# A sparse attention kernel: the next group's lists made in mid-step, TensorE's chain work put ahead of its packing

## The chip, the cores and the metric

The program runs on one core of a Trainium2 chip. The metric is the device time of one execution in microseconds (us). The engines are named as in the profile: PE is TensorE (matmul), PEld its weight loads, DVE is VectorE, ACT ScalarE, POOL GpSimd and SP SyncE, which here only issues DMAs.

## The reference

One layer of graph attention over 8192 nodes with 256 features, 4 heads of 64, and a dense int32 adjacency matrix of 8192 x 8192 (256 MB) in which about 4 entries of a row are one:

```python
h = jnp.maximum(_layernorm(x), 0.0)
support = (h @ weight).reshape(-1, H, D).transpose(1, 0, 2)
f1 = jnp.einsum('hnd,hd->hn', support, weight_u[..., 0])[:, None, :]
f2 = jnp.einsum('hnd,hd->hn', support, weight_v[..., 0])[:, :, None]
masked = jax.nn.leaky_relu(f1 + f2, 0.2) * adj
mask = masked != 0
m = max over the masked entries of a row (0 if there are none)
e = jnp.where(mask, jnp.exp(masked - m), 0)
attn = e / e.sum(axis=2)            # 0 where the sum is 0
out = einsum('hnm,hmd->hnd', attn, support) + bias + h @ proj_w.T + proj_b
return x + out
```

## The kernel before

**The adjacency.** The rows are worked in 64 tiles of 128. SP loads a tile as four **units** of 1 MB (`load_adj`, L317) into a ring of six unit buffers (`HELD`); a new unit may be loaded when PE has used the one six before it (`s_adj_used`). Unit u of tile t is number 4t+u. PE packs each tile into 1024 words per row: two matmuls with a place code (`pack_places`, L392) and four for each unit (`pack_unit`, L400), into one of two PSUM tiles (`ps_words0`, `ps_two`). So a tile can be packed only when DVE has read the tile two before it out of the same PSUM tile. DVE's `pick_words` (L787 and on) takes the 16 largest words of each row; `split_words` (L799 to L813) turns them into neighbour numbers, 16 slots a row.

**First phase (to about 230 us).** For all 64 tiles of rows, layer norm and projections are computed, and the first 17 adjacency tiles (0 to 16) are packed and picked along the way.

**Second phase: steps.** The 64 row tiles are attended to in 32 groups of two. Step g (`for g in range(LATE)`, LATE = 30) has a part on each engine, in an order written out by hand. It works on three groups at once and picks the tiles `picks[g]`, in turn two (even g) and one (odd g) up to step 27, and two in each of steps 28, 29 and 30: step 26 picks 55 and 56, step 27 tile 57, step 28 tiles 58 and 59, step 29 tiles 60 and 61. The pieces, each named by its function:

- For group g+1: DVE `list_own` (L843 to L851; the first five neighbours of each row, and the count of the rest); PE `offsets` (L429, L430); ACT `distances` (L601 to L610).
- For group g: DVE `one_hot` (L859); PE `edge_records` (L438); ACT `record_edges` (L619); DVE `list_spill` (L867 to L877). The rows of a neighbour beyond five ("spill") are handed over by one-hot matmuls.
- For group g-1: DVE `scores` (L885 to L899) once its rows are gathered; PE `row_scores` (L445); DVE `row_maximum` (L908 to L914); PE `edge_refs` (L452); DVE `shift` (L922, L925); ACT `exponential` (L625); DVE `weigh` (L933).
- For group g-2: PE `aggregate` for each of its two tiles (L461, 12 matmuls each); DVE `output` (L939 to L943).

POOL gathers the neighbours' rows of 1040 bytes by indirect DMA (L717), 12 for each group: ten when `list_own` is there and ACT's `clear` (L592) has run, two after `list_spill`. The ring of gathered rows holds three groups.

**Order before the change.** PE in step g: `offsets(g)`; the first two units of the first new tile, which is one tile ahead of the pick; `aggregate(g-2, 0)`, `edge_records(g)`, `row_scores(g-1)`; the other two units; `edge_refs(g-1)`, `aggregate(g-2, 1)`; then the second new tile, if there is one. DVE in step g: pick of the first tile, `one_hot(g)`, `scores(g-1)`, `list_spill(g)`, `row_maximum(g-1)`, `output(g-2, 0)`, pick of the second tile, `shift(g-1)`, `split_words`, `list_own(g+1)`, `output(g-2, 1)`, `weigh(g-1)`.

**End.** The steps LATE and LATE+1 (30 and 31) are written out on their own: the last tile (63) is packed among the chain work of step 30, unit 1 before `aggregate(28, 0)`, unit 2 behind `aggregate(28, 1)`, and unit 3 behind `edge_refs(29)`. SP stores the output (L340) once the last adjacency load is issued.

Of the kernel before, what the change touches and what calls it, by code (L numbers as in the profile page):

```python
# [20 lines left out]
UNITS = 4  # L21
HELD = 6
GS = 2
RING = 3
FIRST = 16
# [18 lines left out]
def gat_kernel(nc, x, adj, weight, weight_u, weight_v, bias, proj_wT, proj_b, out):  # L44
# [4 lines left out]
    TILES = N // P  # L49
# [17 lines left out]
    picks = [list(range(FIRST + sum(counts[:g]), FIRST + sum(counts[:g + 1]))) for g in range(G + 2)]  # L67
    for g in range(1, G - 1):
        assert FIRST + sum(counts[:g]) >= groups[g][0] + groups[g][1]

    gathers = [sum(BLOCKS * groups[q][1] for q in range(g % RING, g + 1, RING)) for g in range(G)]

# [5 lines left out]
    with ExitStack() as ctx:  # L78
# [286 lines left out]
        def _(pe):  # L365
# [19 lines left out]
            def pack_places(t):  # L385

                if buffer_of(t) == 1 and t == FIRST + 1:
                    pe.wait_ge(s_staged, TILES)
                elif t > 0:
                    pe.wait_ge(s_words_seen, t if t <= FIRST else t - 1)  # L390
                for k in range(BANKS):
                    nc.tensor.matmul(ps_words[buffer_of(t)][:, k * 512:(k + 1) * 512], ones_row[:],  # L392
                                     place[:, k * 512:(k + 1) * 512], start=True, stop=False)

            def pack_unit(t, u):
                n = UNITS * t + u
                pe.wait_ge(s_adj_in[n % HELD], 16 * (n // HELD + 1))
                for s in range(UT):
                    for k in range(BANKS):
                        mm = nc.tensor.matmul(ps_words[buffer_of(t)][:, k * 512:(k + 1) * 512],  # L400
                                              pack_w[:, u * UT + s, :], adj_low[:, n % HELD, s, k * 512:(k + 1) * 512],
                                              start=False, stop=(u == UNITS - 1 and s == UT - 1))
                mm.then_inc(s_adj_used, 1)
# [20 lines left out]
            def offsets(g):  # L424
                first, size = groups[g]
                pe.wait_ge(s_spilled, g + 1)
                if g > 0:
                    pe.wait_ge(s_rec_sb, g)
                nc.tensor.matmul(ps_list[:, 0:size], before[:], spilled[:, first:first + size], start=True, stop=True)  # L429
                nc.tensor.matmul(ps_list[:, GS:GS + size], minus_mid[:], spilled[:, first:first + size],  # L430
                                 start=True, stop=True).then_inc(s_offset, 1)

            def edge_records(g):
                first, size = groups[g]
                pe.wait_ge(s_onehot, g + 1)
                pe.wait_ge(s_filed, g + 1)
                for b in range(size):
                    mm = nc.tensor.matmul(ps_rec[:, b], onehot[:, g % 2, b], record[:, first + b, OWN:R_F1],  # L438
                                          start=True, stop=True)
                mm.then_inc(s_rec, 1)  # L440
# [14 lines left out]
            def aggregate(g, b):  # L455
                if g > 0:
                    last, n = groups[g - 1]
                    pe.wait_ge(s_out, last + min(b, n - 1) + 1)
                pe.wait_ge(s_weighted, groups[g][0] + b + 1)
                for k in range(BLOCKS):  # L460
                    mm = nc.tensor.matmul(ps_agg[:, b, 0:ROW], ident[:] if k < OWN else onehotT[:, g % RING, b],  # L461
                                          gathered[:, g % RING, b, k], start=(k == 0), stop=(k == BLOCKS - 1))
                mm.then_inc(s_agg, 1)

            pe.wait_ge(s_staged, TILES)
            for g in range(LATE):
                new = [t + 1 for t in picks[g]]
                offsets(g)
                pack_places(new[0])
                for u in range(UNITS // 2):  # L470
                    pack_unit(new[0], u)
                if g >= 2:
                    aggregate(g - 2, 0)
                edge_records(g)
                if g > 0:
                    row_scores(g - 1)
                for u in range(UNITS // 2, UNITS):
                    pack_unit(new[0], u)
                if g > 0:
                    edge_refs(g - 1)  # L480
                if g >= 2:
                    aggregate(g - 2, 1)
                for t in new[1:]:
                    pack_places(t)
                    for u in range(UNITS):
                        pack_unit(t, u)

            offsets(LATE)
            pack_places(TILES - 1)
# [64 lines left out]
        def _(act):  # L554
# [41 lines left out]
            def distances(g):  # L596
                first, size = groups[g]
                act.wait_ge(s_spilled, g + 1)
                if g > 0:
                    act.wait_ge(s_onehot, g)  # L600
                nc.scalar.activation(reach[:, 0:size], spilled[:, first:first + size], ACT.Square, scale=0.5)  # L601
                nc.scalar.activation(slot_pen[:, g % RING, 0:size], held[:, 0:size], ACT.Copy, scale=-NEG,
                                     bias=NEG).then_inc(s_slot_pen, 1)
                act.wait_ge(s_offset, g + 1)
                n = step(nc.scalar.activation(mid[:, 0:size], ps_list[:, GS:GS + size], ACT.Copy))
                nc.scalar.activation(record[:, first:first + size, R_OFF], ps_list[:, 0:size],
                                     ACT.Copy).then_inc(s_filed, 1)
                act.wait_ge(s_act, n)
                for b in range(size):
                    last = nc.scalar.activation(distance[:, b], edge_odd[:], ACT.Square, scale=0.5,  # L610
                                                bias=mid[:, b:b + 1])
                last.then_inc(s_distance, 1)
# [16 lines left out]
            for g in range(LATE):  # L629
                record_edges(g)  # L630
                if g == 0:

                    for b in range(2):
                        act.wait_ge(s_rows_out[b], 16 * (LOADS // 2))
                    act.wait_ge(s_xhat, TILES)
                    act.wait_ge(s_xT, TILES)
                    act.wait_ge(s_based, TILES)
                    for q in range(RING):
                        clear(q)
                if g > 0:  # L640
                    exponential(g - 1)
                if g + 1 >= RING:
                    clear(g + 1)
                distances(g + 1)

            clear(LATE + 1, 0, 1)
            record_edges(LATE)
# [97 lines left out]
        def _(dve):  # L745
# [36 lines left out]
            def pick_words(t, at):  # L782

                ps = ps_words[buffer_of(t)]
                dve.wait_ge(s_adj_used, UNITS * (t + 1))
                for s in range(CANDS // 8):
                    last = v.max(cand[:, s * 8:(s + 1) * 8], ps[:, s * SEG:(s + 1) * SEG])  # L787
                last.then_inc(s_words_seen, 1)
                dve.wait_ge(s_words_seen, t + 1)
                v.tensor_tensor(seg_top[:], seg_top[:], cand[:, 7::8], ALU.max)  # L790
                after(step(v.max(words[:, at, 0:8], cand[:])))
                after(step(v.match_replace(cand_rest[:], words[:, at, 0:8], cand[:], 0.0)))
                return step(v.max(words[:, at, 8:16], cand_rest[:]))
# [61 lines left out]
            def one_hot(g):  # L855
                size = groups[g][1]
                dve.wait_ge(s_distance, g + 1)
                for b in range(size):
                    last = v.tensor_scalar(onehot[:, g % 2, b], distance[:, b], reach[:, b:b + 1], None, ALU.is_lt)  # L859
                last.then_inc(s_onehot, 1)  # L860
# [85 lines left out]

            list_own(0)
            for g in range(LATE):
                n = pick_words(picks[g][0], 0)
                if g == 0:  # L950

                    dve.wait_ge(s_based, TILES)
                one_hot(g)
                if g > 0:
                    scores(g - 1)
                list_spill(g)
                if g > 0:
                    row_maximum(g - 1)
                if g >= 2:
                    output(g - 2, 0)  # L960
                for t in picks[g][1:]:
                    n = pick_words(t, 1)
                if g > 0:
                    shift(g - 1)
                picked = split_words(picks[g][0], len(picks[g]), n)
                list_own(g + 1)
                if g >= 2:
                    output(g - 2, 1)
                if g > 0:
                    weigh(g - 1)  # L970
# [152 lines left out]
```

## Time and profile before

| | us |
|---|---|
| median of 3 runs | 863.06 |
| lowest, highest | 859.76, 864.25 |
| the profiled execution | 860.12 |
| its span, first to last instruction | 858.4 |

The busy time of each engine over the span: PE 710.9 us (83%), DVE 643.1 (75%), POOL 529.0 (62%), ACT 129.3 (15%). The DMA engines moved 329.82 MB, 384 GB/s in the mean. In a row of the timeline the two numbers ahead are start and duration in us; the bracket is the time for which the engine sat idle before, and what ended it.

### The profile page before, as it was taken

The numbers are of one execution on the slowest core, as the hardware profiler recorded it, in microseconds if no ns is written. First come the engines' busy times: TensorE is split into PE (matmuls) and PEld (weight loads), VectorE is DVE, ScalarE is ACT, GpSimd is POOL, SyncE is SP. The second block draws the span as 40 slices with busy tenths as digits, with TensorE's granted clock in tenths as the row PEclk, the third lists the DMA queues.
The fourth block names the chain that finished last, engine by engine and source line by source line (L and its number), as shares of the span: only waits on it lengthen the run. The fifth ranks groups of instructions, "written<-read, shape, count | busy, mean of one in ns | idle before, by whom it ended". The sixth has DMA issues, their size and how long they took to land.

```text
span 858.4 us, 11157 instructions
## 1 busy us (share of the span) xinstructions
PE 710.9 (83%) x3011; PEld 434.2 (51%) x3011; DVE 643.1 (75%) x2740; ACT 129.3 (15%) x467; POOL 529.0 (62%) x598
## 2 busy tenths in 40 slices
PE   2989999999956878887888888788888878888865
PEld 0656666666513545454555445354544445454454
DVE  4556666657446988879869798977979787886887
ACT  0223333333210111000001011000011100000010
POOL 4344455454467776667766667676766766676570
PEclk9999999999966989888879898887989888988789
DMA  9999999999999999999999999999999999999971
GB/s 307 422 407 393 416 422 416 407 423 413 419 410 384 385 401 402 388 405 384 402 393 374 399 374 405 383 404 384 390 396 375 406 366 400 359 403 401 397 302 53
DMA packets 63855, 329.82 MB, mean 384 GB/s; under 512 B 12795, under 2 KB 15560, under 8 KB 31024
## 3 DMA queue, kind: packets, MB, share of 16 engines
q1 hardware_dynamic: 43056, 286.28, 83.8%
q0 software_dynamic: 18432, 34.30, 11.1%
q10 hardware_dynamic: 2304, 8.52, 2.4%
q8 instruction: 25, 0.41, 0.2%
q14 instruction: 38, 0.31, 0.1%
HBM read 328.99 MB, written 16.91 MB: 403 GB/s over the span
## 4 chain that ended last, share of the span: by engine, by line
PE 42%; DMA 25%; DVE 24%; issue 4%; POOL 3%; ACT 1%; POOLq 0%; ACTq 0%; SPq 0%
DMA adj_raw<-in_adj 21%; PE ps_words L400 11%; PE ps_agg L461 9%; PE ps_agg L381 7%; PE ps_two L381 6%; DVE att L933 5%; PE ps_two L400 5%; DVE cand L787 3%; DVE base L943 3%; POOL att L717 2%; DMA att<-support_table,idx 2%; PE ps_score L445 2%; DMA att<-in_x 1%; PE ps_words L392 1%; DMA support_table<-att 1%
## 5 line engine op out<-in xcount | busy, mean ns | idle before, releaser
L717 POOL DMA_INDIRECT att<-support_table,idx x384 | 417.4, 1087 | 188.7 <-issue 105.8
L400 PE MATMUL ps_words<-adj_raw,pack_w 128*128 128x512 fp8e4 x640 | 186.7, 428 | 25.4 <-DMA adj_raw<-in_adj 25.3
L461 PE MATMUL ps_agg<-att,ident 128*128 128x260 f32 x640 | 176.3, 428 | 8.5 <-DVE att L933 8.5
L461 PEld LDWEIGHTS ps_agg<-att,ident 128*128 128x128 f32 x640 | 135.1, 218 | 41.6 <-issue 18.6
L400 PE MATMUL ps_two<-adj_raw,pack_w 128*128 128x512 fp8e4 x384 | 118.9, 457 | 24.6 <-DMA adj_raw<-in_adj 24.5
L400 PEld LDWEIGHTS ps_words<-adj_raw,pack_w 128*128 128x128 bf16 x640 | 62.1, 106 | 125.3 <-DMA adj_raw<-in_adj 39.8
L787 DVE MAX8 cand<-ps_words 128x8 f32<-128x128 f32 x320 | 67.1, 281 | 66.3 <-PE ps_words L400 66.3
L933 DVE TENSOR_TENSOR att<-att 128x1536 f32<-128x1536 f32 x64 | 109.4, 1750 | 0.4 <-ACT att L625 0.4
L708 POOL COPY record<-att 128x8 f32<-128x8 f32 x64 | 13.4, 209 | 117.4 <-ACT att L569 117.4
L400 PEld LDWEIGHTS ps_two<-adj_raw,pack_w 128*128 128x128 bf16 x384 | 38.7, 113 | 91.5 <-DMA adj_raw<-in_adj 40.0
L381 PE MATMUL ps_agg<-w_all,hT 128*128 128x260 f32 x256 | 63.0, 389 | 4.1 <-ACT hT L565 4.1
L381 PE MATMUL ps_two<-w_all,hT 128*128 128x260 f32 x256 | 62.6, 388 | 3.0 <-ACT hT L565 3.0
L943 DVE SCALAR_TENSOR_TENSOR base<-ps_agg,rdenom,base 128x64 f32<-128x64 f32 x256 | 55.0, 277 | 2.3
L381 PEld LDWEIGHTS ps_two<-w_all,hT 128*128 128x128 f32 x256 | 47.8, 192 | 11.9 <-ACT hT L565 3.5
L381 PEld LDWEIGHTS ps_agg<-w_all,hT 128*128 128x128 f32 x256 | 46.0, 190 | 13.5 <-ACT hT L565 7.9
L706 POOL TENSOR_TENSOR base<-att,bias_row 128x256 f32<-128x256 f32 x64 | 46.8, 732 | 0.1
L710 POOL TENSOR_TENSOR base<-base,att 128x256 f32<-128x256 f32 x64 | 46.6, 729 | 0.0
L867 DVE TENSOR_SCALAR edge_slot<-edge_rec,edge_at 128x2 f32<-128x2 f32 x32 | 7.8, 245 | 51.2 <-ACT edge_rec L619 51.2
L787 DVE MAX8 cand<-ps_two 128x8 f32<-128x128 f32 x192 | 40.2, 280 | 6.6 <-PE ps_two L400 6.5
L619 ACT ACTIVATE edge_rec<-ps_list 128x34 f32<-128x34 f32 x32 | 6.4, 199 | 243.3 <-PE ps_list L438 243.2
L445 PE MATMUL ps_score<-score_slot,onehotT 128*128 128x44 f32 x128 | 24.6, 331 | 19.7 <-DVE score_slot L899 19.6
L625 ACT ACTIVATE att<-shifted 128x24 f32<-128x24 f32 x64 | 10.7, 215 | 189.9 <-DVE shifted L925 189.9
(118 smaller groups left out, 821.2 us busy)
## 6 DMA issues: line engine op xcount, KB each, us to landing
adj_raw<-in_adj SPq DMA_DIRECT2D x256, 1024.0 KB, 13.3
support_table<-att ACTq DMA_DIRECT2D x16, 520.0 KB, 8.8
att<-in_x SPq DMA_DIRECT2D x16, 512.0 KB, 6.7
out<-base SPq DMA_DIRECT2D x15, 512.0 KB, 14.1
att<-support_table,idx POOLq DMA_INDIRECT x384, 6.2
out<-base SPq DMA_DIRECT2D x4, 128.0 KB, 1.9
w_all<-in_proj_wT SPq DMA_DIRECT2D x2, 128.0 KB, 6.0
w_all<-in_weight SPq DMA_DIRECT2D x2, 128.0 KB, 6.3
```

The lines of the kernel that those rows point to most:

```text
L381: mm = nc.tensor.matmul(ps_proj[t % 2][:, half, 0:ROW], hT[:, t % 2, c * P:(c + 1) * P], w_all[:, c, half, :], start=(c == 0), stop=(c == ...
L400: mm = nc.tensor.matmul(ps_words[buffer_of(t)][:, k * 512:(k + 1) * 512], pack_w[:, u * UT + s, :], adj_low[:, n % HELD, s, k * 512:(k + 1 ...
L445: mm = nc.tensor.matmul(ps_row[:, b].rearrange("p k h -> p (k h)"), onehotT[:, g % RING, b], score_slot[:, b].rearrange("p k h -> p (k h)" ...
L461: mm = nc.tensor.matmul(ps_agg[:, b, 0:ROW], ident[:] if k < OWN else onehotT[:, g % RING, b], gathered[:, g % RING, b, k], start=(k == 0) ...
L625: last = nc.scalar.activation(gathered[:, g % RING, b, :, HF:], shifted[:, b], ACT.Exp)
L706: pool.tensor_tensor(base[:, t], x_in[:, g % 2, q, :], bias_row[:], ALU.add).then_inc(s_basev, 1)
L708: pool.tensor_copy(record[:, t, R_F2:].rearrange("p (a h) -> p a h", a=2), stage[:, g % 2, :, q, HF:])
L710: pool.tensor_tensor(base[:, t], base[:, t], stage[:, g % 2, 0, q, 0:HF], ALU.add).then_inc(s_based, 1)
L717: pool.indirect_dma_start(gathered[:, g % RING, b, k, :], None, table, bass.IndirectOffsetOnAxis(idx[:, g % RING, b, k:k + 1], 0), bounds_ ...
L787: last = v.max(cand[:, s * 8:(s + 1) * 8], ps[:, s * SEG:(s + 1) * SEG])
L933: v.tensor_tensor(r, r, rows[:, :, HF:].unsqueeze(3).to_broadcast([P, BLOCKS, H, HD]), ALU.mult).then_inc(s_weighted, 1)
L943: last = v.scalar_tensor_tensor(base[:, t, cols], ps_agg[:, b, cols], rdenom[:, b, h:h + 1], base[:, t, cols], ALU.mult, ALU.add)
```

## The change

DVE makes the list of the next group (`list_own(g+1)`) in the middle of a step instead of near its end, and `one_hot(g)` is the first thing in a step; PE makes `offsets(g+1)` in step g, and ACT the distances ahead of the exponential. This holds for the groups in `AHEAD`, which the formula makes groups 1 to 26; groups 0 and 27 to 29 keep the old place, and steps 30 and 31 are as before. PE packs tile 17 before the first step, and in every step does all the chain work first and then packs the tiles two ahead of those that DVE picks in that step: step 28 packs 60 and 61, step 29 packs 62.

```diff
+    AHEAD = [g for g in range(1, LATE) if FIRST + sum(counts[:g - 1]) >= groups[g][0] + GS]
...
             pe.wait_ge(s_staged, TILES)
+            pack_places(FIRST + 1)
+            for u in range(UNITS):
+                pack_unit(FIRST + 1, u)
             for g in range(LATE):
-                new = [t + 1 for t in picks[g]]
-                offsets(g)
-                pack_places(new[0])
-                for u in range(UNITS // 2):
-                    pack_unit(new[0], u)
+                if g not in AHEAD:
+                    offsets(g)
+                if g in AHEAD:
+                    edge_records(g)
                 if g >= 2:
                     aggregate(g - 2, 0)
-                edge_records(g)
+                if g not in AHEAD:
+                    edge_records(g)
                 if g > 0:
                     row_scores(g - 1)
-                for u in range(UNITS // 2, UNITS):
-                    pack_unit(new[0], u)
+                if g >= 2:
+                    aggregate(g - 2, 1)
                 if g > 0:
                     edge_refs(g - 1)
-                if g >= 2:
-                    aggregate(g - 2, 1)
-                for t in new[1:]:
-                    pack_places(t)
-                    for u in range(UNITS):
-                        pack_unit(t, u)
+                if g + 1 in AHEAD:
+                    offsets(g + 1)
+                for t in picks[g]:
+                    if t + 2 < TILES - 1:
+                        pack_places(t + 2)
+                        for u in range(UNITS):
+                            pack_unit(t + 2, u)
...
-                if g > 0:
+                if g > 0 and g + 1 not in AHEAD:
                     exponential(g - 1)
                 if g + 1 >= RING:
                     clear(g + 1)
                 distances(g + 1)
+                if g > 0 and g + 1 in AHEAD:
+                    exponential(g - 1)
...
             list_own(0)
             for g in range(LATE):
+                if g in AHEAD:
+                    one_hot(g)
                 n = pick_words(picks[g][0], 0)
...
-                one_hot(g)
+                if g in AHEAD:
+                    list_spill(g)
+                else:
+                    one_hot(g)
                 if g > 0:
                     scores(g - 1)
-                list_spill(g)
+                if g not in AHEAD:
+                    list_spill(g)
+                if g + 1 in AHEAD:
+                    list_own(g + 1)
                 if g > 0:
                     row_maximum(g - 1)
...
                 picked = split_words(picks[g][0], len(picks[g]), n)
-                list_own(g + 1)
+                if g + 1 not in AHEAD:
+                    list_own(g + 1)
```

## Rows read from the trace of the kernel before

**Rows 1.** The page, parts 1 and 3: busy us by engine; packets, MB and share of a queue.
```profile
PE 710.9 (83%) x3011; PEld 434.2 (51%) x3011; DVE 643.1 (75%) x2740; ACT 129.3 (15%) x467; POOL 529.0 (62%) x598
...
q0 software_dynamic: 18432, 34.30, 11.1%
```

**Rows 2.** Busy time by stretch; behind it the granted clock, DMA share and GB/s.
```profile
core 0: us, PE busy (x) PEld busy (x) DVE busy (x) ACT busy (x) POOL busy (x), PEclk, DMA share, GB/s
60.00:230.00 170.00, 166.69 (x781) 113.06 (x780) 103.96 (x441) 54.49 (x121) 85.36 (x162) 1.00 1.01 414
290.00:800.00 510.00, 423.10 (x1747) 250.53 (x1745) 423.86 (x1817) 50.96 (x264) 351.80 (x323) 0.87 1.00 391
830.00:840.00 10.00, 6.61 (x35) 5.78 (x34) 7.83 (x34) 0.53 (x3) 5.54 (x6) 0.95 0.38 128
```

**Rows 3.** Adjacency loads, issue to landing, in 290 to 800 us.
```profile
DMA to landing us min/median/max: 9.6/15.3/19.4
```

**Rows 4.** The same, in 60 to 230 us.
```profile
DMA to landing us min/median/max: 7.7/9.1/11.2
```

**Rows 5.** The chain that ended last: start, us, what (a landing, then PE's work on it).
```profile
430.00 13.34 DMA adj_raw<-in_adj
...
443.39 1.89 PE ps_words L400 x4
...
771.08 14.52 DMA adj_raw<-in_adj
785.64 1.89 PE ps_two L400 x4
787.53 3.91 PE ps_agg L461 x12
...
794.10 15.05 DMA adj_raw<-in_adj
809.20 1.89 PE ps_two L400 x4
811.08 4.08 PE ps_agg L461 x12
```

**Rows 6.** Timeline of steps 29 and 30, DVE's pieces by their first instruction.
```profile
792.06 0.23 DVE L867 TENSOR_SCALAR edge_slot<-edge_rec,edge_at 128x2 f32<-128x2 f32 x1 [5.78 <-ACT edge_rec L619]
...
793.44 0.24 DVE L908 TENSOR_TENSOR row_score<-ps_score,slot_pen 128x88 f32<-128x88 f32 x1
...
795.39 1.67 DVE L787 MAX8 cand<-ps_two 128x8 f32<-128x128 f32 x8
...
797.90 0.18 DVE L922 TENSOR_TENSOR shifted<-row_score,row_ref 128x40 f32<-128x40 f32 x1
798.08 0.17 DVE L799 CAST words_i<-words 128x32 int32<-128x32 f32 x1
...
801.50 0.18 DVE L843 TENSOR_SCALAR held<-record 128x22 f32<-128x22 f32 x1
...
802.98 3.42 DVE L933 TENSOR_TENSOR att<-att 128x1536 f32<-128x1536 f32 x2
...
805.61 0.69 ACT L610 ACTIVATE distance<-edge_odd,mid 128x128 f32<-128x128 f32 x2
...
806.32 1.67 DVE L787 MAX8 cand<-ps_words 128x8 f32<-128x128 f32 x8
...
811.35 0.47 DVE L859 TENSOR_SCALAR onehot<-distance,reach 128x128 f32<-128x128 f32 x2
...
812.83 0.25 DVE L899 TENSOR_TENSOR score_slot<-slot_hot,score 128x88 f32<-128x88 f32 x1
```

**Rows 7.** Timeline of DVE from `list_spill(30)` to the pick of tile 63.
```profile
815.78 0.23 DVE L867 TENSOR_SCALAR edge_slot<-edge_rec,edge_at 128x2 f32<-128x2 f32 x1 [2.70 <-ACT edge_rec L619]
...
819.96 0.16 DVE L925 TENSOR_TENSOR shifted<-score,ps_score 128x8 f32<-128x8 f32 x1 [0.67 <-PE ps_score L452]
...
821.22 0.88 DVE L787 MAX8 cand<-ps_two 128x8 f32<-128x128 f32 x4
```

## The prediction

> **What bounds the kernel now.** I read the busy times first: no engine is full (PE 83%, DVE 75%) [rows 1]. The stretches then tell why: in the first phase and in the second, up to about 830 us, the DMA share is 1.00 or 1.01 of the 16 engines' time, whatever PE and DVE do; it falls to 0.38 only in 830 to 840 us [rows 2]. The chain of waits agrees: in the second phase its long pieces are adjacency landings, of 12 to 15 us each, with one unit of packing and the first `aggregate` of a step behind them [rows 5]. Tile 34 unit 1 (number 137) is there at 443.4 us and tile 61 unit 1 (number 245) at 785.6: 108 units in 342.2 us, 3.17 us each, so a pair of steps (three tiles, 12 units) takes 38.0 us. That is the pace of the loads. They are never short of requests: from issue to landing a unit takes 15.3 us in the median and 9.6 at least [rows 3], which at 3.17 us each is about five in flight and three at the least. In the first phase it is 9.1 us [rows 4] at 1.05 MB / 414 GB/s = 2.5 us a unit, hence about 3.6, and the rate was higher there; so five in flight are more than are needed.
>
> The time is therefore: loads at full pace until the last unit (809.2 us for number 253, 2.94 us each since number 245, so number 255 at about 815) [rows 5], and then the chain work that can't be done before. I look at the change from these two sides.
>
> **The change in the loop, groups 1 to 26.** It adds and removes no instruction, no byte and no gather; all is moved. DVE has the list of the next group some 8 us earlier in a step, and the distances are ready when the step begins, so `one_hot` waits for nothing. PE's waiting for data moves from between two chain pieces to the end of a step. This would be a gain if DVE or PE set the pace. They don't, so I price the loop at nothing, with the loads as its cover. The cover has to be looked at, since the new order uses some of it up.
>
> DVE: from `list_spill` to the end of `weigh`, a step that picks two tiles takes 792.06 to 806.32 without a wait, 14.3 us; the next pick, `split_words`, list and `one_hot` end at 811.82 and `scores` at 813.08 [rows 6]. Within it a pick is 2.5 us (795.39 to 797.90) and `split_words` of two tiles 3.4 (798.08 to 801.50). A two-pick step is then 14.3 + 2.5 (first pick) + 0.5 (`one_hot`) + 1.25 (`scores`) = 18.5 us, and a one-pick step 2.5 less for the pick and about 1.2 less for the split, 14.8 us. The pair is 33.3 us. To it come waits that the new order puts in: `edge_records` and ACT's copy behind PE's last packing (0.8 us), and `edge_refs` now behind both aggregates (about 1.5 us in the one-pick step). Some 36 us against 38.0: covered, with 2 us to spare.
>
> Loads: PE now does not pack from the end of one step's tile until the next step's chain is through. After a one-pick step that is longest: `one_hot` is late there, and then come two aggregates and the small matmuls, in my count 13 to 14 us. In that time 4 units land, of at most 6 asked for, so about 1.5 stay in flight where before there were three at the least. The first phase shows full rate at about three. That 1.5 is enough is not shown by any row. Lower bound of this cost 0; upper bound: a full landing less the cover, say 1 us for each of 13 pairs, 13 us. I take 0, since 1.5 units are still 4.7 us of transfer when the next request goes out, and add it to the range.
>
> The queues: SP issues the same loads in the same order, only up to 10 us later each. POOL's 12 gathers of a group are issued from earlier indices; nothing waited for the gathers but a microsecond or so. ACT's exponential moves behind about 1.1 us of distances, with `split_words` and `output` between it and `weigh`: nothing.
>
> **The change at the end, steps 27 to 29.** Here is the term that I count. These groups are not ahead: their list is made late in a step, and `offsets(g)` comes first on PE in step g. But in the new order PE reaches step g only after it has packed two tiles ahead. Before, the chain work of step 29 (first aggregate 787.5 us) ran when unit 1 of tile 61 had landed [rows 5]. Now PE must have packed all of tile 61 in step 28: unit 3 lands at 785.64 + 2 x 2.94 = 791.5 us. From that landing it goes as before from unit 1 (packing 1.89 us, aggregate 3.9, edge records, ACT), which took 785.64 to 792.06 = 6.4 us, plus 0.3 for `offsets(29)` that stands between: `list_spill(29)` at 798.2 instead of 792.06, **6.1 us later**. The distances are then not what ends it: ACT has them 1.2 us after the offsets, `one_hot` and `scores` are done by 797 to 798. From there DVE has the same unbroken 14.3 us to the end of `weigh(28)`, and 6.8 more to the end of `scores(29)`: 813.08 + 6.1 = 819.2. In the old order DVE waited 2.70 us there for PE, which was then behind with its aggregate [rows 7]. In the new one the aggregate is done by then (PE packs 62 by 808 and needs `list_own(30)`, 807.6), and `edge_records(30)` waits only for `one_hot(30)` at 817.9. So 2.6 us of the delay are swallowed and `list_spill(30)` comes at 819.3, 3.5 us late. But `row_scores(29)` now starts only at 819.2, with `aggregate(28, 1)` (2.9 us), unit 2 of tile 63 (1.0) and `edge_refs(29)` behind it: `shift` can end at about 824.4 instead of 819.96, 4.5 us late, and the pick of tile 63 at 825.7 instead of 821.22 [rows 7]. From that pick on, the old chain is DVE and PE hand to hand to the end, with no load in it, so the 4.5 us stay.
>
> Against it stands one thing. Since the chain lags by 9 us or so at that point, about 6 fewer gathers have gone out when tile 61 lands. A gather is 0.09 MB (the software queue's 34.30 MB [rows 1] over 384 of them), 0.23 us at 391 GB/s, so the adjacency units come 6 x 0.23 = 1.4 us earlier. DVE's `scores(28)` then becomes the later of the two, so that not all of it counts. Bounds for the end: 2.5 us (all of it counts, and PE's aggregate at the higher of its two clock levels) to 6.1 (nothing is swallowed). I take 4.0.
>
> **Sum.** Loop 0, start of the second phase 0 (DVE stands there for the first gathers and the loads go on), end +4.0. Against the profiled execution's 860.12 us that is 864.1. The median of the runs shown is 2.9 us above it, and I put the sum on that: 863.06 + 4.0 = 867.1 us, +0.46%. About 0.5% (4.3 us) is what a measurement of this kernel can tell from no change, and the sum is just inside it.
>
> **Rivals.**
> *Slower by more: the loop loses its cover.* The place is the two-pick step after a one-pick step: if the loads run dry between PE's pauses, or DVE's 36 us and its waits come to more than 38.0 us, each pair grows. For it: three in flight become 1.5, and the spare is 2 us. Against it: the DMA engines also have the gathers, and a pair can be late once and catch up. It decides from a pause of PE of about 16 us on. At 0.3 to 1.3 us a pair, 13 pairs: 4 to 17 us on top, 871 to 884 us. Chance 0.20.
> *Faster: the DMA share is no limit.* The row shows 391 GB/s in 290 to 800 us against 414 in the first phase at the same share of 1.00 [rows 2]. If late and uneven requests make the difference, and lists made earlier even them out, up to 510 x (1 - 391/414) = 28 us are there; I would expect a third or less, 3 to 9 us, less the 4 of the end: 855 to 862 us. Against it: the gathers' small descriptors are in the second phase in either order, and PE asks for units in longer bursts. Chance 0.15. The Trainium skill (Perfetto Trace Analysis, Identifying the Most-Contended Engine) speaks for this rival: it says that the occupancy of the 16 DMA engines misleads and that the HBM utilization should be read in its place. By that rule my cover is not proved and the kernel should gain where its chain gets shorter; the trace bears it out as far as that the rate differs by 6% between stretches of equal share.
> *No change: the delay at the end is swallowed.* If DVE's and PE's small waits in steps 30 and 31 take up more than I found, the last store is where it was, 862 to 864 us. Chance 0.10.
>
> **How the numbers follow.** My forecast has 0.55; since 4.0 is so near 4.3, it counts 0.30 within 0.5% and 0.25 slower. The first rival adds 0.17 slower and 0.03 within, the second 0.15 faster, the third 0.10 within. Faster 0.15, same 0.43, slower 0.42. The range: 858 leaves out the deeper half of the faster rival, 879 the last of the slower one.
>
> **What would show it.** Right: DMA share 1.00 and 38 us a pair in 290 to 800 us; issue to landing at a median below 15.3 us and a least below 9.6; number 255 at 813 to 816 us; `list_spill(29)` at about 798 and the pick of tile 63 at about 826 us. Wrong: a share below 0.98 in the loop or a pair above 38.5 us (first rival); above 395 GB/s and a pair under 37.5 us (second); the pick of 63 before 823 us (third).

## The result and the profile after

The changed kernel is slower. Its median is 869.54 us (22 runs, 862.29 to 873.11), that of the kernel before 861.14 us (22 runs, 859.13 to 864.25): a ratio of 1.0088, 95% interval 1.0072 to 1.0104, or +7.6 us. The range of the prediction holds it. The direction was the one forecast at +0.46%, and the size is nearly twice that.

The page of the changed kernel, parts 1 and 3:
```profile
span 871.4 us, 11157 instructions
PE 705.7 (81%) x3011; PEld 443.8 (51%) x3011; DVE 644.9 (74%) x2740; ACT 124.1 (14%) x467; POOL 541.3 (62%) x598
...
q0 software_dynamic: 18432, 34.30, 10.9%
```
The instructions and bytes are the same in number as before [rows 1]. The traced execution took 873.11 us, at the upper end of its runs; the trace before was of one near the median. So of the 13.0 us between the two spans, only some 8 are the usual difference. One more thing is needed to read the numbers below: in two sets of runs the kernel before itself took 873 us (set A: the first `lists_only`, `order_only`, a first run of both repairs, `after_again`) and 874 us (set B: `before_warm`, `lists_only_b`), and executions clearly slower than the rest of their kernel (one of `held7_before` and one of `two_between` took over 2 ms) are left out of the ratios.

Stretches of the changed kernel, columns as in [rows 2]; the last but one is a stretch of 6 us that I picked out:
```profile
60.00:230.00 170.00, 166.68 (x780) 112.76 (x780) 103.47 (x437) 53.90 (x119) 85.73 (x163) 1.00 1.01 414
290.00:800.00 510.00, 407.98 (x1716) 250.30 (x1715) 419.18 (x1779) 45.68 (x260) 360.08 (x320) 0.88 0.98 386
552.00:558.00 6.00, 6.00 (x29) 3.54 (x28) 5.59 (x27) 1.51 (x9) 4.49 (x5) 0.90 0.49 144
829.80:871.40 41.60, 25.07 (x97) 20.19 (x97) 28.65 (x108) 2.04 (x11) 12.16 (x11) 0.79 0.29 104
```
The first phase is unchanged. In the loop the DMA share is 0.98 instead of 1.00 and the rate 386 GB/s instead of 391. What is missing lies in short spells: in 552 to 558 us the DMA engines are half idle. The same bytes at 386 instead of 391 GB/s take 510 x (391/386 - 1) = 6.6 us more; this is of one execution, the slowest of the 22, and the traces further on show how much of it is usual. The loads' time from issue to landing (290 to 800 us):
```profile
DMA to landing us min/median/max: 7.4/15.1/19.1
```
The least is 7.4 us, where it was 9.6 [rows 3]. At 3.2 us a unit that is, by my estimate, at times only two requests in flight, not three.

PE around that spell, from the timeline of the changed kernel:
```profile
537.44 3.77 PE L402 MATMUL ps_two<-adj_raw,pack_w 128*128 128x512 fp8e4 x16
...
544.07 0.62 PE L440 MATMUL ps_list<-record,onehot 128*128 128x17 f32 x4 [2.85 <-DVE onehot L868]
...
549.71 4.13 PE L463 MATMUL ps_agg<-att,ident 128*128 128x260 f32 x10
...
555.13 3.77 PE L402 MATMUL ps_words<-adj_raw,pack_w 128*128 128x512 fp8e4 x16
```
It is the even step behind an odd one. PE packs until 541.2 us, waits 2.85 us for DVE's `one_hot`, does both aggregates (the second partly at the lower clock, 4.13 us where 2.44 is usual), and packs again only from 555.13: a pause of 13.9 us, in which no unit buffer comes free. The usual long pause of a pair of steps is 12.2 us. It grows, to 13.9 us at most, where the second aggregate, not the first, is the one at the lower clock, since behind the first one PE has 1.83 us of waiting for `score_slot` in which the delay is lost. This trace has three pauses of 13.9 us (from 350.2, 541.2 and 619.7 us).

DVE at the end, the rows that answer to [rows 6, 7]:
```profile
801.12 0.23 DVE L876 TENSOR_SCALAR edge_slot<-edge_rec,edge_at 128x2 f32<-128x2 f32 x1 [1.94 <-ACT edge_rec L626]
...
815.37 1.68 DVE L796 MAX8 cand<-ps_words 128x8 f32<-128x128 f32 x8
...
822.07 0.22 DVE L876 TENSOR_SCALAR edge_slot<-edge_rec,edge_at 128x2 f32<-128x2 f32 x1
...
828.51 0.16 DVE L934 TENSOR_TENSOR shifted<-score,ps_score 128x8 f32<-128x8 f32 x1 [2.94 <-PE ps_score L454]
829.77 0.88 DVE L796 MAX8 cand<-ps_two 128x8 f32<-128x128 f32 x4
```
`list_spill(29)` comes at 801.12 instead of 792.06 (+9.1), `list_spill(30)` at 822.07 instead of 815.78 (+6.3), the pick of tile 63 at 829.77 instead of 821.22 (+8.6). What ended the wait ahead of step 29 is the last unit of tile 61, at 794.5 us:
```profile
794.48 1.89 PE L402 MATMUL ps_two<-adj_raw,pack_w 128*128 128x512 fp8e4 x4 [1.38 <-DMA adj_raw<-in_adj]
796.16 0.21 PE L431 MATMUL ps_list<-spilled,before 128*128 128x2 bf16 x1
...
796.26 3.80 PE L463 MATMUL ps_agg<-att,ident 128*128 128x260 f32 x10
...
800.33 0.52 PE L440 MATMUL ps_list<-record,onehot 128*128 128x17 f32 x4
```

### The profile page after: what moved, and what is told of

The parts are those of the page before. It is cut to its first block, busy times and chain, and to the rows that moved or that the text cites. A ratio compares the mean times of both kernels' runs of the same rounds, so it can differ in the third digit from the quotient of the medians.

```text
span 871.4 us, 11157 instructions
## 1 busy us (share of the span) xinstructions
PE 705.7 (81%) x3011; PEld 443.8 (51%) x3011; DVE 644.9 (74%) x2740; ACT 124.1 (14%) x467; POOL 541.3 (62%) x598
## 4 chain that ended last, share of the span: by engine, by line
PE 50%; DVE 23%; DMA 18%; issue 3%; POOL 3%; ACT 1%; POOLq 0%; ACTq 0%; SPq 0%
PE ps_agg L463 18%; DMA adj_raw<-in_adj 15%; PE ps_words L402 10%; PE ps_agg L383 7%; PE ps_two L383 6%; DVE att L942 6%; PE ps_two L402 3%; DVE cand L796 3%; DVE base L952 2%; PE ps_score L447 2%; POOL att L726 2%; PE ps_words L394 1%; DMA att<-in_x 1%; PE ps_score L454 1%; PE ps_list L440 1%
## 5 line engine op out<-in xcount | busy, mean ns | idle before, releaser
L726 POOL DMA_INDIRECT att<-support_table,idx x384 | 429.2, 1118 | 186.2 <-issue 108.7
L463 PE MATMUL ps_agg<-att,ident 128*128 128x260 f32 x640 | 202.7, 477 | 4.9 <-DVE att L942 4.9
L402 PE MATMUL ps_words<-adj_raw,pack_w 128*128 128x512 fp8e4 x640 | 173.9, 409 | 29.8 <-DMA adj_raw<-in_adj 29.7
L463 PEld LDWEIGHTS ps_agg<-att,ident 128*128 128x128 f32 x640 | 148.6, 241 | 33.3 <-issue 5.4
L402 PE MATMUL ps_two<-adj_raw,pack_w 128*128 128x512 fp8e4 x384 | 103.3, 414 | 37.1 <-DMA adj_raw<-in_adj 36.8
L402 PEld LDWEIGHTS ps_words<-adj_raw,pack_w 128*128 128x128 bf16 x640 | 59.1, 100 | 127.6 <-DMA adj_raw<-in_adj 42.3
L402 PEld LDWEIGHTS ps_two<-adj_raw,pack_w 128*128 128x128 bf16 x384 | 34.4, 100 | 101.1 <-DMA adj_raw<-in_adj 51.7
L440 PE MATMUL ps_list<-record,onehot 128*128 128x17 f32 x128 | 21.4, 283 | 33.1 <-DVE onehot L868 33.1
L440 PEld LDWEIGHTS ps_list<-record,onehot 128*128 128x128 f32 x128 | 22.4, 230 | 44.4 <-DVE onehot L868 40.2
L463 PE MATMUL ps_agg<-att,onehotT 128*128 128x260 f32 x128 | 40.5, 400 | 0.0
```

Source lines behind the costliest of these rows:

```text
L726: pool.indirect_dma_start(gathered[:, g % RING, b, k, :], None, table, bass.IndirectOffsetOnAxis(idx[:, g % RING, b, k:k + 1], 0), bounds_ ...
```

## The experiments

Three theories. **End**: step 29's chain waits for all of tile 61, so the last steps are late (the term of my sum). **Loop**: PE's pauses let the loads run low (my first rival). **Clock**: PE runs at its lower clock behind the pick of 63, since from that pick to the end the changed kernel's trace has 871.4 - 829.8 = 41.6 us and the one before 858.4 - 821.2 = 37.2. All ratios are to the kernel before on the same chip. The edits are against the changed kernel unless said.

**The end alone.** Steps 28 and 29 get PE's order of before; step 27 packs nothing, to fall back from two tiles ahead to one.
```diff
-            for g in range(LATE):
+            for g in range(28):
...
-                    if t + 2 < TILES - 1:
+                    if t + 2 < 59:
...
+            for g in range(28, LATE):
+                new = [t + 1 for t in picks[g]]
+                offsets(g)
+                pack_places(new[0])
...
```


> The changed kernel, but step 27 packs nothing and steps 28 and 29 have PE's order of before (one tile ahead, half of it before the chain work). End theory (the chain of step 29 waits for all of tile 61): list_spill(29) comes back from 801.1 us to some 795 to 796, the pick of tile 63 from 829.8 to 824 or 825, and 4 to 5 us of the 8 go: ratio to before 1.003 to 1.005. Loop theory alone (the loads run dry in the loop, and everything behind is shifted): ratio stays at 1.008 to 1.010, and the idle spells of the DMA stay in either case. Clock theory (PE at its lower clock in the last 25 us makes the difference): the pick of 63 moves but the time does not.

Measured: 865.27 us, ratio 1.0039 (1.0021 to 1.0056). The end theory gave 1.003 to 1.005. DVE's rows in this kernel:
```profile
788.90 0.22 DVE L898 TENSOR_SCALAR edge_slot<-edge_rec,edge_at 128x2 f32<-128x2 f32 x1
...
811.80 0.23 DVE L898 TENSOR_SCALAR edge_slot<-edge_rec,edge_at 128x2 f32<-128x2 f32 x1 [0.51 <-ACT edge_rec L648]
...
817.24 0.88 DVE L818 MAX8 cand<-ps_two 128x8 f32<-128x128 f32 x4
```
`list_spill(29)` at 788.9 and the pick of 63 at 817.2 are 12 us earlier than in the changed kernel. That is more than expected (795 and 824), and earlier even than before; the traced execution was the fastest (858.65 us), so I go by the ratio: the repair is worth 0.49% or 4.2 us.

**One more unit buffer**, in the changed kernel and in the one before.
```diff
-HELD = 6
+HELD = 7
```

> The changed kernel with seven unit buffers instead of six, so that one more load is always asked for. Loop theory: PE's pauses of 13 to 15 us no longer empty the queue, the DMA share in 290 to 800 us goes from 0.98 to 1.00 and the rate from 386 to 390 GB/s or more, the loop's end comes 3 us earlier, and the ratio to before is 1.003 to 1.006. End theory alone: nothing changes, 1.008 to 1.010.

> The kernel before with seven unit buffers. Both theories: three units in flight at the least were enough, so a seventh buffer gives nothing: ratio 0.998 to 1.001. If more requests in flight raised the rate by themselves (the DMA share being no limit), it would be 0.99 or less.

Measured: 1.0067 (1.0046 to 1.0089) for the changed kernel, 1.0003 (0.9985 to 1.0021) for the one before. The stretches of the changed kernel with seven buffers, and its landings:
```profile
290.00:800.00 510.00, 408.01 (x1750) 250.71 (x1749) 423.74 (x1805) 46.21 (x261) 359.34 (x323) 0.88 0.99 391
```
```profile
DMA to landing us min/median/max: 9.3/17.4/22.7
```
The rate is that of before again, 391 GB/s, and the least time to landing is back from 7.4 to 9.3 us. The time gained is 0.21% (1.8 us), under the expected 0.3 to 0.6%, and the interval holds the changed kernel's 1.0088: by itself this gain is not shown. Nor did the dry spells end. Of the two pauses of 13.9 us in this trace one has a spell as deep as those with six buffers:
```profile
514.00:520.00 6.00, 6.00 (x31) 3.25 (x29) 5.59 (x29) 1.51 (x9) 4.59 (x5) 0.98 0.45 127
```
With six buffers (the changed kernel, `end_old`, and `after_warm` below) all six pauses of 13.9 us have such a stretch of 6 us, at a share of 0.43 to 0.50; with seven (here and with both repairs, below) three of five do, at 0.42 to 0.50, and the other two stay at 0.72 and 0.75. In the two traces of the old order no stretch of 6 us is under 0.80. So the spells belong to the new order; the seventh buffer softens some of them. The kernel before gains nothing from more requests, which also speaks against my rival of a DMA share that is no limit.

**Both repairs.** The edit of `end_old` and `HELD = 7`.

> The changed kernel with both repairs, seven unit buffers and the old order in steps 27 to 29, a second time (in the first job with it the kernel before itself took 870 us and more, and engines stood for 10 us with nothing in the program to wait for). The same expectations: if the two causes add up, ratio 1.000 to 1.003; if PE's lower clock behind the pick of 63 is a third and lasting part, 1.003 or more with over 40 us from that pick to the end.

Measured: 860.89 us, ratio 1.0007 (0.9990 to 1.0024), inside the 1.000 to 1.003 expected. The two repairs together take 0.81% of the 0.88%; the seventh buffer's part beside the end repair is 0.32% (1.0039 against 1.0007, measured on two chips, the intervals just overlapping). The same kernel in set A had 1.0604, far outside the same expectation. With an unchanged program that shows how far a ratio of set A can be off.

**Two units between the chain pieces.** I tried to shorten the pause in another way: of each step's first tile, two units packed before `row_scores`.
```diff
                 if g >= 2:
                     aggregate(g - 2, 0)
...
+                first = picks[g][0] + 2
+                if first < TILES - 1:
+                    pack_places(first)
+                    for u in range(UNITS // 2):
+                        pack_unit(first, u)
                 if g > 0:
                     row_scores(g - 1)
```


> The changed kernel with two units of the first tile packed between aggregate(g-2, 0) and row_scores(g-1), in every step; tiles are still packed two ahead and the lists made in mid-step. Loop theory: the longest gap between two requests falls from 15 us to 10 or 11, the DMA's idle spells of 1 us and more go, ratio 1.003 to 1.006. End theory alone: no gain, and up to 2 us more in step 29, where row_scores(28) then waits for unit 1 of tile 62: 1.008 to 1.012.

Measured: 897.08 us, ratio 1.0406 (1.0377 to 1.0435). No theory had it. What DVE waited for in 290 to 760 us, first this kernel (in total, times, longest), then the changed kernel:
```profile
DVE row_score L923 <- PE ps_score L447: 75.7, 23, 4.1
DVE shifted L940 <- PE ps_score L454: 10.7, 12, 0.9
DVE edge_slot L882 <- ACT edge_rec L632: 1.3, 1, 1.3
```
```profile
DVE edge_slot L876 <- ACT edge_rec L626: 31.6, 12, 6.2
DVE row_score L917 <- PE ps_score L447: 18.7, 24, 1.9
DVE shifted L934 <- PE ps_score L454: 10.7, 12, 0.9
```
In the changed kernel DVE stands 31.6 us in 12 pairs of steps at `edge_slot`, behind PE that waits for data: 2.6 us a pair is all that the hand-to-hand chain has to spare under the loads. The two units cost PE 2.6 us (places 0.6, units 2.0) twice a pair, right ahead of `row_scores`. That is 5.2 us against 2.6: the wait at `edge_slot` is gone (1.3 us), `row_maximum` waits 3.3 us each time, and the chain sets the pace. The 2.6 us that are too much, in 13 pairs, are 34 us; the kernel is some 27 us slower than the changed one (1.0406 against 1.0088). The whole stretch runs at 368 GB/s:
```profile
290.00:800.00 510.00, 393.72 (x1625) 248.41 (x1624) 392.58 (x1685) 44.28 (x250) 331.33 (x299) 0.84 0.94 368
```

**PE's order without the early lists.** `AHEAD = []`, in set A.

> PE's order of the change (chain first, two tiles ahead) with no group ahead: every step is as steps 27 to 29 are in the change. Each step that PE enters from a wait for data then has offsets and distances between that data and list_spill, some 4 us once a pair: the hand-to-hand chain of a pair is 36.1 us in the changed kernel (38.7 less the 2.6 us that DVE waits at list_spill) and becomes 39 to 40. End and loop theories: 1.02 to 1.04. If the early lists did nothing for the chain: as the change, 1.008 to 1.010.

Measured: 912.42 us, ratio 1.0446 (1.0378 to 1.0515), above the expected 1.02 to 1.04. But in this same set both repairs together gave 1.0604, where elsewhere they gave 1.0007, so this ratio can't be told from what the set adds. That two tiles ahead without the early lists is worse than with them is argued (the expectation counts 3 to 4 us more in the chain of a pair), not shown.

**The early lists without PE's order**, in set A and in set B. PE's part of the edit, against the kernel before:
```diff
-                offsets(g)
+                if g not in AHEAD:
+                    offsets(g)
                 pack_places(new[0])
                 for u in range(UNITS // 2):
                     pack_unit(new[0], u)
+                if g in AHEAD:
+                    edge_records(g)
...
                 if g >= 2:
                     aggregate(g - 2, 1)
+                if g + 1 in AHEAD:
+                    offsets(g + 1)
```


> The lists, offsets, distances and one_hot early for groups 1 to 26 as in the change, but PE packs one tile ahead and half of it before the chain work, as before. If the change's loss comes from PE's order and the two tiles ahead (loop and end theories), nothing is lost here: ratio 0.998 to 1.002, pairs of 38.0 us, the pick of 63 at 820 to 823 us. If mid-step lists were themselves a gain that the packing order hides: 0.997 or less. If they were themselves the loss (DVE does list_spill ahead of scores and stands in it for PE): 1.005 or more, with row_maximum waiting for row_scores.

> The early lists alone, with PE's packing as before, a second time (the first was in the job whose kernel before took 870 us and more, with a 14 us stand of DVE and ACT at 266 us that nothing in the program explains). From the first trace: PE never waits for data in the loop, DVE and PE go hand to hand at 38.3 us a pair against 38.0 before, since DVE stands in list_spill ahead of scores and edge_refs comes behind two units. So 1.002 to 1.005. If mid-step lists were a gain of their own: 0.998 or less.

Measured: 1.0139 (1.0088 to 1.0190) and 1.0081 (1.0034 to 1.0127), both above what I had expected (0.998 to 1.002, then 1.002 to 1.005). Both traces hold a stand of DVE and ACT at the start of the second phase; in the second one:
```profile
276.82 0.16 DVE L936 TENSOR_TENSOR shifted<-score,ps_score 128x8 f32<-128x8 f32 x1 [13.15 <-remote]
281.02 0.17 ACT L614 ACTIVATE mid<-ps_list 128x2 f32<-128x2 f32 x1 [18.80 <-remote]
```
PE had finished what they needed by 266.7 us, and I found nothing in the program that holds them; `before_warm`, in set B too, has such a stand of 9.7 us at the same instruction. Its cause stays open. Behind it, in 290 to 760 us, PE hardly waits for data:
```profile
PE ps_list L440 <- DVE onehot L870: 63.2, 24, 5.8
...
PE ps_words L402 <- DMA adj_raw<-in_adj: 1.9, 4, 0.7
```
and the rate is 389 GB/s. So there is no sign that the early lists by themselves speed up the loop. Whether they cost anything of their own stays open.

**PE kept busy at the end.** 22 matmuls that compute nothing of use, in three gaps behind the last packing.
```diff
+            def keep_busy(n):
+                for _ in range(n):
+                    nc.tensor.matmul(ps_words0[:, 0:512], before[:], pack_w[:, 0:4, :], start=True, stop=True)
...
+            pe.wait_ge(s_words_seen, TILES - 1)
+            keep_busy(12)
             offsets(LATE + 1)
...
+            keep_busy(7)
             aggregate(LATE, 0)
             row_scores(LATE + 1)
+            keep_busy(3)
```


> The changed kernel with matmuls that compute nothing of use in three gaps of PE behind the last packing: 12 ahead of offsets(31), 7 ahead of aggregate(30, 0), 3 behind row_scores(31), each of 512 columns. They take away nothing but PE's idle time there. Clock theory: the aggregates of the last 30 us run at the higher clock (2.9 us for 12 matmuls, where they took 4.5 to 5.5), the time from the pick of 63 to the end falls from 41.6 us to 36 or 37, and the ratio to before from 1.009 to 1.003 or 1.005. End and loop theories alone: ratio stays at 1.008 to 1.010, or grows by up to 2 us where the added matmuls stand in the way.

Measured: 864.50 us, ratio 1.0046 (1.0024 to 1.0068), and 861.9 - 824.6 = 37.3 us from the pick of 63 to the end, both as the clock theory had it. `aggregate(30, 0)` and what follows, first the changed kernel, then this one:
```profile
848.38 4.67 PE L463 MATMUL ps_agg<-att,ident 128*128 128x260 f32 x10 [3.34 <-DVE att L942]
...
856.44 4.10 PE L463 MATMUL ps_agg<-att,ident 128*128 128x260 f32 x10
```
```profile
839.90 1.46 PE L497 MATMUL ps_words<-pack_w,before 128*128 128x512 bf16 x6
843.16 2.43 PE L463 MATMUL ps_agg<-att,ident 128*128 128x260 f32 x10 [1.81 <-DVE att L950]
...
848.63 2.44 PE L463 MATMUL ps_agg<-att,ident 128*128 128x260 f32 x10
```
Behind 3.34 us of idling the same ten matmuls took 4.67 us; with the gap filled they took 2.43. The idling right before is not all of it, though: in the trace of before the same matmuls took 2.43 us behind as long a gap.
```profile
839.66 2.43 PE L461 MATMUL ps_agg<-att,ident 128*128 128x260 f32 x10 [3.40 <-DVE att L933]
```
The mean granted clock from the pick of 63 to the end is 0.79 in the changed kernel, 0.95 in this one, and 0.91 in the trace of before.

This trace also shows the changed kernel's loop once more, since the added matmuls all come behind the pick of 63:
```profile
789.35 1.89 PE L402 MATMUL ps_two<-adj_raw,pack_w 128*128 128x512 fp8e4 x4 [1.60 <-DMA adj_raw<-in_adj]
...
795.93 0.23 DVE L884 TENSOR_SCALAR edge_slot<-edge_rec,edge_at 128x2 f32<-128x2 f32 x1 [1.92 <-ACT edge_rec L634]
...
824.57 1.67 DVE L804 MAX8 cand<-ps_two 128x8 f32<-128x128 f32 x8
```
With six buffers, a rate of 387 GB/s and two pauses of 13.9 us, the last unit of tile 61, `list_spill(29)` and the pick of 63 all come some 5 us earlier than in the changed kernel's own trace. With seven buffers the last two are at 796.2 and 824.8 us, no earlier. So those 5 us are of that one slow execution and not of the change.

**The control for it**, in set B: the same matmuls in the kernel before.

> The kernel before with the same added matmuls behind its last packing (12, 7 and 3 of 512 columns). It is the control for the clock theory: what they take from the kernel before is no part of the difference between the two kernels. In the changed kernel they took 0.42 per cent. If the lower clock at the end is the changed kernel's own trouble: ratio 0.999 to 1.001. If the kernel before has it too, in some executions or in part of the time: 0.996 to 0.998, and 37 us from the pick of 63 to the end in every case; the clock is then no cause of the difference, or only the rest of 0.42 less this.

Measured: 0.9971 (0.9921 to 1.0022), inconclusive. What the other traces say of the end, from the pick of 63 to the last instruction: 41.6 and 41.7 us in the changed kernel and in `held7`; 39.7 and 861.2 - 819.6 = 41.6 with the end repair (`end_old`, both repairs); 37.2 and 40.0 in the two traces of the old order (before, `held7_before`). The time follows the granted clock of that stretch: 0.79 wherever it is 41.6 or 41.7, 0.83 at 39.7 and 40.0, 0.91 at 37.2. The kernel with both repairs has as slow an end as the changed one and is as fast as the kernel before, but its pick of 63 came 0.6 to 1.6 us earlier than in the two traces of the old order, which makes up for a part. So the filled gaps are worth about 0.4% of the changed kernel; that the change brought the lower clock is not shown, and neither is that it didn't. `after_again`, meant to settle this with a second trace, fell into set A (976.77 us) and says nothing.

No version run was shown to beat the kernel before.

## Why the prediction was right, and where it was not

*Loads bound the loop.* Right. 391 GB/s and 1.00 before; with seven buffers no gain.

*The end, +4.0 us.* Right, and by the mechanism named: removing it gave 4.2 us, and the pick of 63, forecast 4.5 us late, is 3.4 us late in `after_warm` (824.6 against 821.2) and 4.7 in `held7` against `held7_before` (824.8 against 820.1). That 4.2 meets 4.0 so well is in part luck, since the end repair is not the exact reverse of this term: in its two traces the pick of 63 comes even up to 4 us earlier than before. In the changed kernel's trace PE waits for unit 3 of tile 61 until 794.5 us; `list_spill(29)` follows 6.6 us behind that landing, where I had 6.7. I had put the landing at 791.5, so the 3 us by which the step is later than forecast come from the loop of that execution; in `after_warm` PE packs that unit at 789.4 us and the step comes at 795.9, 6.6 us behind again. The part that was to be swallowed was too: +9.1 us at `list_spill(29)`, +6.3 at `list_spill(30)`, 2.8 less, where I had 2.6. From there to the pick of 63 another 2.3 us were added against my 1.0, since `aggregate(28, 1)` ran at the lower clock and took 4.6 us in place of 2.9.

*The loop, 0.* The argument for this term failed: "I take 0, since 1.5 units are still 4.7 us of transfer when the next request goes out". The pause was rightly counted (13 to 14 us; measured 12.2 and at times 13.9), but the loads do run low in it, and in the longer ones the DMA engines are half idle for 6 us. What decides between the two lengths, which of the two aggregates runs at PE's lower clock, I had not thought of. As a size, 0 was not far off. In the slowest execution the loop lost some 5 us; in `after_warm`, with the same loop, the loads are as early at the end as with seven buffers. In the timed runs the seventh buffer returned 0.21% alone and 0.32% beside the end repair, 1.8 to 2.8 us, the first of them not clear of noise and the second barely. The first rival named this, was too dear with its 4 to 17 us on top, and set the pause that decides too long, at 16 us. The two terms together, 0.81%, are the measured difference of 0.88% within its interval.

*The gathers' delay, 1.4 us earlier loads.* Not told apart by any run.

*The cover of DVE, 2 us a pair.* Right by the trace (2.6 us), and `two_between` showed what lies beyond it. My own experiment overran the bound that I had worked out before.

*The faster rival.* It didn't happen. The kernel before, given more requests, ran at 1.0003, so the lower rate of the second phase is not for want of requests. I had set a rule beside it, that the occupancy of the DMA engines misleads (the Trainium skill, Perfetto Trace Analysis, Identifying the Most-Contended Engine). Here the share of 1.00 did mark the bound. A share of 0.98 or 0.99 over the loop told little of the time: `after_warm`, at 0.99, had its loads no later than before. What the same section would have one read instead, the HBM utilization, I did not use, so the rule as a whole is not tested.

*PE's clock at the end.* It was in my bounds for one aggregate only. It moves the end of single executions by 4 us and makes, together with the dry spells in the loop, the changed kernel's runs spread over 11 us, or so I take it; the spread itself has no experiment.

## What to carry to other kernels

Where the loads set the pace, an order that gives a compute engine more slack gained nothing in the loop here, and it had two prices: buffers stay occupied through longer pauses (small, and different from execution to execution), and the last tiles' dependent work starts one tile later (4 us). Look at what the first chain piece of the last steps waits for, and count the buffers against the longest pause, with the engine at its lower clock. Before moving work between two engines that hand results to and fro, compare it with the wait that the loads leave in that chain: 2.6 us a pair was all there was, and with 5.2 us the kernel was 3% slower. And compare the trace with a second one of the same program before putting down a difference of a few us to the change: the one trace of the changed kernel was 5 us late by itself.

## What was unexpected of the hardware

The time to landing did not tell the dry spells well. In the first phase a least of 7.7 us goes with 414 GB/s [rows 2, 4], in the changed kernel's loop a least of 7.4 us with 386. In `end_old` the least is 5.1 us, with 388 GB/s and only one pause of 13.9 us. What told them was the DMA share of short stretches: 0.49 in the 6 us around the end of a pause. The deep spells come from PE: one aggregate at its lower clock (4.13 us instead of 2.44), if it is the second of a pause, makes the pause 1.7 us longer and leaves the DMA engines short of requests. And filling PE's idle gaps with useless matmuls made the changed kernel 0.42% faster.
